# Packed score columns, quarter-wide states and y tiles in a state-space scan with FFN on one core

## The reference

```python
# B=4 sequences, L=512 tokens, D=256; NH=32 heads of HEADDIM=8, D_STATE=64
h = layernorm(x) * (1 + ca) + sa
xBC, z, A_log = split(h @ W_in.T)            # x: 256, B: 32*64, C: 32*64, z: 256, A: 32
xBC = causal depthwise conv of 4 taps (xBC) + conv_b
a = -softplus(A_log)
Lm = exp(segsum(a))                          # lower triangle, per head 512 x 512
M = einsum('blhn,bshn,bhls->bhls', Cm, Bm, Lm)
y = einsum('bhls,bshp->blhp', M, x) + D * x
x = x + ga * ((y * silu(z + z_bias)) @ W_out.T)
h = layernorm(x) * (1 + cb) + sb
x = x + gb * (fwht(silu(h @ W1.T) * (h @ W3.T)) @ W2.T)
```

## Time and profile before

| | us |
|---|---|
| median of 3 runs | 563.15 |
| lowest, highest | 562.98, 563.3 |
| the profiled execution | 562.82 |
| its span, from the first to the last instruction | 561.0 |

### The profile page before, as it was taken

How to read it: one execution, slowest core, us unless ns; L and a number is a source line. 1 busy time by engine, 2 the same in 40 slices (tenths; PEclk the granted TensorE clock), 3 DMA queues, 4 the chain that set the end, 5 groups by cost and what they waited for, 6 DMA issues and landing times.

```text
span 561.0 us, 18569 instructions
## 1 busy us (share of the span) xinstructions
PE 551.6 (98%) x6701; PEld 447.0 (80%) x6702; DVE 471.9 (84%) x746; ACT 392.3 (70%) x988; POOL 256.8 (46%) x523
## 2 busy tenths in 40 slices
PE   7999999999999999999999999999999999999997
PEld 4577787888778878788887888787788988889887
DVE  7899999999999999999999999999948637647343
ACT  2679898898898888988988989988723323333240
POOL 4854387576577577687678364656100000000000
PEclk9899999999999999999999999999999999999999
DMA  8636534433433535533533437456741042100101
GB/s 275 264 140 199 171 120 132 166 117 121 168 117 118 168 112 203 171 113 119 162 127 117 143 142 223 135 163 191 204 136 54 22 129 75 39 2 0 39 1 37
DMA packets 40816, 72.01 MB, mean 128 GB/s; under 512 B 4676, under 2 KB 12100, under 8 KB 40520
## 3 DMA queue, kind: packets, MB, share of 16 engines
q1 hardware_dynamic: 40776, 71.52, 40.0%
HBM read 57.34 MB, written 13.12 MB: 126 GB/s over the span
## 4 chain that ended last, share of the span: by engine, by line
PE 93%; DVE 2%; issue 2%; POOL 1%; DMA 1%; ACT 0%; SPq 0%; POOLq 0%; DVEq 0%; ACTq 0%
PE ps L355 20%; PE ps L357 20%; PE ps L356 20%; PE ps L530 9%; PE ps L512 5%; PE ps L574 5%; PE ps L549 4%; PE ps L565 4%; PE ps L640 2%; PE ps L449 1%; PE ps L377 1%; PE ps L407 1%; PE ps L421 1%; PE ps L650 1%; DMA u_sb<-in_u 1%
## 5 line engine op out<-in xcount | busy, mean ns | idle before, releaser
L1148 DVE SCALAR_TENSOR_TENSOR acc<-ps,cw_dve,acc 128x511 f32<-128x511 f32 (+2 forms) x384 | 257.7, 742 | 2.9 <-ACT acc L807 2.7
L839 ACT ACTIVATE decay<-sums,p_slot 128x128 f32<-128x128 f32 x512 | 161.1, 399 | 4.8 <-POOL sums L1436 2.1
L1432 POOL TENSOR_SCALAR_AFFINE_SELECT sums<-sums 128x512 f32<-128x512 f32 x128 | 82.4, 644 | 93.5 <-DMA sums<-running_sums 88.5
L807 ACT ACTIVATE acc<-ps,cw_act 128x512 f32<-128x512 f32 x128 | 93.1, 776 | 32.2 <-PE ps L574 30.1
L355 PE MATMUL ps<-ht_hi,wg_hi 128*128 128x512 f32 x256 | 107.1, 418 | 0.0
L356 PE MATMUL ps<-ht_lo,wg_hi 128*128 128x512 f32 x256 | 101.2, 395 | 0.0
L357 PE MATMUL ps<-ht_hi,wg_lo 128*128 128x512 f32 x256 | 101.1, 395 | 0.0
L1136 DVE TENSOR_TENSOR mix<-ps,decay 128x1024 f32<-128x1024 f32 x64 | 78.2, 1222 | 11.4 <-PE ps L530 10.2
L974 ACT ACTIVATE silu_sb<-ps 128x512 f32<-128x512 f32 x32 | 19.2, 599 | 77.8 <-PE ps L357 77.8
L1436 POOL TENSOR_SCALAR_AFFINE_SELECT sums<-sums 64x256 f32<-64x256 f32 x128 | 51.9, 405 | 29.7 <-POOL sums L1432 29.2
L1366 POOL TENSOR_TENSOR rstd<-vareps,minus_half 128x4 f32<-128x4 f32 x8 | 8.4, 1047 | 120.4 <-DVE vareps L1030 116.8
(11 more groups left out here) (142 smaller groups left out, 945.2 us busy)
## 6 DMA issues: line engine op xcount, KB each, us to landing
sums<-running_sums SPq DMA_DIRECT2D x128, 256.0 KB, 3.2
y_parts<-yt_sb SPq DMA_DIRECT2D x32, 256.0 KB, 2.0
wg_raw<-in_w_bc SPq DMA_DIRECT2D x8, 512.0 KB, 4.5
stage<-y_parts SPq DMA_DIRECT2D x16, 256.0 KB, 4.5
u_sb<-in_u SPq DMA_DIRECT2D x4, 512.0 KB, 4.3
stage<-in_w SPq DMA_DIRECT2D x1, 2048.0 KB, 13.2
x_channels<-acc SPq DMA_DIRECT2D x8, 256.0 KB, 2.6
ee<-decay_rows SPq DMA_DIRECT2D x8, 256.0 KB, 3.9
```

The costliest lines, as they stand in the source:

```text
L807: af(acc[:, b % 2, t, :], ps[:, PROJ_BANK[t], :], ACT.Identity, bias=cw_act[:, t, 1:2], scale=cw_act[:, t, 0:1]).then_inc(s[f"tap_a{t}"], 1)
L839: i = af(decay[:, j, c * P:(c + 1) * P], sums[:, j, c * P:(c + 1) * P], ACT.Exp, scale=-1.0, bias=p_slot[:, b * CH + c, j:j + 1])
L1148: stt(a[:, d:], ps[:, PROJ_BANK[t], 0:L - d], cw_dve[:, t, TAPS - 1 - d:TAPS - d], a[:, d:], ALU.mult, ALU.add).then_inc(s[f"taps{t}"], 1)
L1432: gp.affine_select(out=v, in_=v, compare_op=ALU.is_ge, fill=FAR, base=0, pattern=[[0, 2], [NS, 2], [1, P]], channel_multiplier=-1).then_in ...
```

## The change

Masks, scores, decays and `mix` take 384 columns a head instead of 512. The first 64 targets of a chunk have only its first 64 sources; the other 64 partitions of their columns were masked. Two chunks, an even and an odd one, now share PW = 192 columns: in partitions 0 to 63 stand first the 64 columns of the odd chunk's second sources, then the 128 of the even chunk's first sources, and in partitions 64 to 127 the same with even and odd exchanged. `sums_d` gets two packed rows of 384 a head, one for each half of the partitions, in four DMAs at the start. What is above the diagonal is always within 64 columns of a half, so a mask is one addition of a constant tile `far_above`, 0 or 3e38, to 256 columns (no select).

y takes 256 columns of bank 7 instead of 512: for a pair of chunks k and a pair of heads p, `intra` writes 32 partitions in quarter 2 k + p, and `inter` 32 in quarter 2 (1 - k) + p, both in columns 128 k to 128 k + 127. So quarters 0 and 1 take two matmuls of `inter`, quarters 2 and 3 one, and each takes four of `intra`. `xs` becomes a row of weight blocks in which a window of 32 columns has the head's x in its place and zeros elsewhere. `inter` takes the states of two heads in one matmul of 32 columns, 6 instead of 12. `intra` has 16 as before, 32 wide, 8 of 128 and 8 of 64 columns. `states` has 24 matmuls on quarters of 32 state rows instead of 12 on halves of 64. `own_x` is four products with a 0/1 column in place of two copies. `store_y` is two DMAs and `load_y` eight, of 128 columns each, instead of two of 512. The matrices `triu`, `strict` and `ones`, which nothing reads, are no longer loaded.

```diff
+PW = P + NS
+PL = CH // 2 * PW
+XW = 4 * QD + HD
+ST0 = [0, 48, 64]
...
+            packed = sums_d.rearrange("(n h) (k m) -> n h k m", h=2, k=2)
+            full = sums_t[:].rearrange("p (k e l) -> p k e l", k=2, e=2)
+            for h in range(2):
+                sp.dma_start(packed[:, h, :, NS:PW], full[:, :, h, :]).then_inc(s["st_sums"], 16)
+                sp.dma_start(packed[:, h, :, 0:NS], full[:, :, 1 - h, NS:P]).then_inc(s["st_sums"], 16)
+            sp.wait_ge(s["st_sums"], 64)
...
-                row = sums_d[bass.ds(b * NH + g * JH + j, 1), :]
-                sp.dma_start(sums[:, j, :], row.to_broadcast([P, L])).then_inc(s[f"ld_sum{j}"], 16)
+                rows = sums_d[bass.ds((b * NH + g * JH + j) * 2, 2), :].unsqueeze(1)
+                sp.dma_start(sums[:, j, 0:PL], rows.to_broadcast([2, NS, PL])).then_inc(s[f"ld_sum{j}"], 16)
 
             def store_y(g, b):
 
                 sp.wait_ge(s["yt_ev"], g * B + b + 1)
-                sp.dma_start(y_d[bass.ds((b * NG + g) * P, P), :], yt_sb[:, b % 2, :]).then_inc(s[f"st_y{b % 2}"], 16)
+                for h in range(2):
+                    rows = y_d[bass.ds(((2 * b + h) * NG + g) * NS, NS), :]
+                    sp.dma_start(rows, yt_sb[NS * h:NS * (h + 1), b % 2, :]).then_inc(s[f"st_y{b % 2}"], 16)
...
             def load_y(b, kt):
 
-                own = y_d[(b * NG + 4 * kt) * P:(b * NG + 4 * kt + 4) * P, :].rearrange("(q r) l -> q r l", r=QD)
-                load(yi[:, kt, :], own[:, 0:HD, :], f"ld_y{kt}")
-                load(yo[:, kt, :], own[:, HD:2 * HD, :], f"ld_y{kt}")
+                for part, dst in enumerate((yi, yo)):
+                    for c in range(CH):
+                        k, r = divmod(c, 2)
+                        first = ((2 * b + (part ^ k)) * NG + 4 * kt) * NS
+                        own = y_d[first:first + 4 * NS, k * P:(k + 1) * P].rearrange("(q r x) l -> r q x l", r=2, x=2 * HD)
+                        load(dst[:, kt, c * P:(c + 1) * P], own[r], f"ld_y{kt}")
...
-                            i = mm(ps[NS * at:NS * (at + 1), 2 + a, c * P + NS * h:(c + 1) * P],
+                            o = c // 2 * PW + NS * (1 - h)
+                            i = mm(ps[NS * at:NS * (at + 1), 2 + a, o:o + P - NS * h],
...
+                        for i4 in range(JH):
+                            j = 2 * p + i4 // 2
+                            own = slice(QD * i4, QD * (i4 + 1))
                             o = ps[own, 6, 3 * P + p * 24 + c * HD:3 * P + (p + 1) * 24]
-                            i = mm(o, b_tok[:, p, c * P + NS * a:c * P + NS * (a + 1)],
+                            i = mm(o, b_tok[:, p, c * P + QD * i4:c * P + QD * (i4 + 1)],
...
-                for c in range(1, CH):
-                    for j in range(JH):
-                        p, a = divmod(j, 2)
-                        mm(ps[QD * j:QD * j + YW, 7, c * P:(c + 1) * P], st_sb[:, p, a, c - 1, :],
-                           acc[:, b % 2, 2 + p, c * P:(c + 1) * P], start=(c == 1), stop=False, skip_group_check=True)
+                for c in (2, 1, 3):
+                    for p in range(2):
+                        k = c // 2
+                        quarter = 2 * (1 - k) + p
+                        mm(ps[QD * quarter:QD * (quarter + 1), 7, k * P:(k + 1) * P], st_sb[:, p, ST0[c - 1]:ST0[c - 1] + QD],
+                           acc[:, b % 2, 2 + p, c * P:(c + 1) * P], start=(c < CH - 1), stop=False, skip_group_check=True)
 
             def intra(q, b):
 
-                pe.wait_ge(s["xs_done"], 2 * q + 2)
+                pe.wait_ge(s["xs_done"], 4 * q + 4)
                 pe.wait_ge(s["mixed"], 2 * q + 2)
-                for c in range(CH):
-                    for j in range(JH):
-                        i = mm(ps[QD * j:QD * j + YW, 7, c * P:(c + 1) * P], xs[:, b % 2, c, j, :],
-                               mix[:, j, c * P:(c + 1) * P], start=False, stop=True, skip_group_check=True)
-                        if c == CH - 1:
-                            i.then_inc(s["intra"], 1)
+                for a in range(2):
+                    for h in range(2):
+                        for k in (1, 0):
+                            for p in range(2):
+                                j = 2 * p + a
+                                quarter = 2 * k + p
+                                w = j * XW - HD * a + (2 * k + h) * QD
+                                i = mm(ps[QD * quarter:QD * (quarter + 1), 7, k * P + NS * h:(k + 1) * P],
+                                       xs[:, b % 2, w:w + QD], mix[:, j, k * PW + NS * (1 - h):k * PW + PW - P * h],
+                                       start=False, stop=True, skip_group_check=True)
+                                if a and h:
+                                    i.then_inc(s["intra"], 1)
...
+                for n in range(CH):
+                    k, h = divmod(n, 2)
+                    own = slice(k * PW + NS * (1 - h), k * PW + PW - P * h)
+                    i = af(decay[:, j, own], sums[:, j, own], ACT.Exp, scale=-1.0, bias=p_slot[:, b * CH + n, j:j + 1])
...
-                nc.scalar.copy(yt_sb[:, half, :], ps[:, 7, :]).then_inc(s["yt_ev"], 1)
+                    act.wait_ge(s[f"st_y{half}"], 32 * before)
+                nc.scalar.copy(yt_sb[:, half, :], ps[:, 7, 0:2 * P]).then_inc(s["yt_ev"], 1)
...
-                tt(mix[:, 2 * p:2 * p + 2, :], ps[:, 2:4, :], decay[:, 2 * p:2 * p + 2, :],
+                tt(mix[:, 2 * p:2 * p + 2, 0:PL], ps[:, 2:4, 0:PL], decay[:, 2 * p:2 * p + 2, 0:PL],
...
+            gp.memset(far_above[:], 0.0).then_inc(s["mask_set"], 1)
+            gp.memset(own_half[:], 0.0).then_inc(s["mask_set"], 1)
+            for h in range(2):
+                rows = slice(NS * h, NS * (h + 1))
+                pool.wait_ge(s["mask_set"], 2 + 2 * h)
+                gp.memset(own_half[rows, h:h + 1], 1.0).then_inc(s["mask_set"], 1)
+                gp.affine_select(out=far_above[rows], in_=far_above[rows], compare_op=ALU.is_ge, fill=FAR, base=0,
+                                 pattern=[[1, NS]], channel_multiplier=-1).then_inc(s["mask_set"], 1)
+            pool.wait_ge(s["mask_set"], 6)
...
-                even = x_tok[:, b * CH:(b + 1) * CH:2, bass.ds(g * GC, GC)]
-                odd = x_swapped[:, b, :, bass.ds(g * GC, GC)]
-                gp.tensor_copy(xs[:, b % 2, 0::2, :, 0:HD], even.rearrange("p c (j e) -> p c j e", j=JH)).then_inc(s["xs_done"], 1)
-                if isinstance(n, int) and n < B:
-                    pool.wait_ge(s[f"ld_xs{b}"], 32)
-                gp.tensor_copy(xs[:, b % 2, 1::2, :, 0:HD], odd.rearrange("p c (j e) -> p c j e", j=JH)).then_inc(s["xs_done"], 1)
+                blocks = xs[:, b % 2, :].rearrange("p (j w) -> p j w", j=JH)[:, :, 0:4 * QD].rearrange("p j (k w) -> p k j w", k=2)
+                for c in range(2):
+                    if c == 0:
+                        x = x_tok[:, b * CH:(b + 1) * CH:2, bass.ds(g * GC, GC)]
+                    else:
+                        x = x_swapped[:, b, :, bass.ds(g * GC, GC)]
+                        if isinstance(n, int) and n < B:
+                            pool.wait_ge(s[f"ld_xs{b}"], 32)
+                    x = x.rearrange("p k (j e) -> p k j e", j=JH)
+                    for h in range(2):
+                        at = QD * h + 2 * HD * c
+                        rows = own_half[:, (h + c) % 2:(h + c) % 2 + 1].unsqueeze(1).unsqueeze(1).to_broadcast([P, 2, JH, HD])
+                        gp.tensor_tensor(blocks[:, :, :, at:at + HD], x, rows, ALU.mult).then_inc(s["xs_done"], 1)
 
             def mask(n, j):
 
                 await_unit(f"ld_sum{j}", 16 * (n + 1))
-                v = sums[:, j, :].rearrange("p (c e l) -> p c e l", c=2, e=2)
-                gp.affine_select(out=v, in_=v, compare_op=ALU.is_ge, fill=FAR, base=0, pattern=[[0, 2], [NS, 2], [1, P]],
-                                 channel_multiplier=-1).then_inc(s["masked"], 1)
-                await_unit("masked", 8 * n + 2 * j + 1)
-                o = v[0:NS, :, 1, :]
-                gp.affine_select(out=o, in_=o, compare_op=ALU.is_ge, fill=FAR, base=-NS, pattern=[[0, 2], [1, P]],
-                                 channel_multiplier=-1).then_inc(s["masked"], 1)
+                v = sums[:, j, 0:PL].rearrange("p (k l) -> p k l", k=2)[:, :, 0:P].rearrange("p k (e l) -> p k e l", e=2)
+                far = far_above[:].unsqueeze(1).unsqueeze(1).to_broadcast([P, 2, 2, NS])
+                gp.tensor_tensor(v, v, far, ALU.add).then_inc(s["masked"], 1)
```

More of the change, by code:

```diff
@@ L61, in adaln_ssm_ffn_kernel @@
         x_tok = sb("x_tok", [P, TT, D], F32)
-        cst = sb("cst", [P, 5, P], F32)
-        ident, triu, strict, ones, hadamard = (cst[:, i, :] for i in range(5))
+        cst = sb("cst", [P, 2, P], F32)
+        ident, hadamard = (cst[:, i, :] for i in range(2))
         wo_sb = sb("wo_sb", [P, KT, D], F32)
@@ L428, in p_transposes @@
                 for c in range(CH):
-                    if c % 2 == 0:
```

(28 more changed lines are left out.)

53 lines of the change are left out of this document (26 added, 27 removed).

## The result

The changed kernel takes **794.35 us** (median of 4 runs, 792.76 to 795.9) against 563.07 us for the kernel before in the same series: a ratio of 1.411 (95% interval 1.4075 to 1.4146). The forecast was 545.7 us, range 539.5 to 554. It is wrong by far, and its sign too. The profiled execution took 792.76 us, its span is 791.0 us.

What follows compares the result with a forecast made beforehand. TensorE was taken as the bound, VectorE and ScalarE close behind. 30 steps x 0.62 = 18.6 us, plus 0.6 in the tail, less 1.8 for loads of y, gave 17.4 us gained: 545.7 us, range 539.5 to 554.

Steps and rivals of the forecast that it cites:

- SP and DMA: SP's queue and transfers: one more y store issue, sums stored in four DMAs, some 2 us later; cost nil.
- rival 3: SP's queue: small y loads take 0.6 us each and land late, costing 8 us instead of 1.8; 552 us, chance 0.08.
- Inter and intra: TensorE's `inter` and `intra` blocks: the busiest quarters go from 1.54 to 1.12 us a step, gain 0.42.
- States: TensorE's `states` block, 24 matmuls for 12: 0.60 us instead of 0.80, gain 0.20 a step; bounds 0.47 and 1.49.
- rival 1: TensorE's `states`: matmul records cost time wherever they go, 29 ns each gives 573 us, 22 ns gives 563; chance 0.09.
- The step: TensorE's step in the loop: from 10.68 to 10.06 us, above VectorE's 9.8 and ScalarE's 8.9.
- VectorE: VectorE's `mix` products, 768 columns for 1024: 0.24 us saved on each, its step falls from 10.3 to 9.8 us.
- rival 2: VectorE or ScalarE bounds the step: if `mix` saves nothing, the step is 10.35 us, the time 554 us; chance 0.13.
- GpSimd: GpSimd's masks and `own_x` products: a mask 0.74 us instead of 1.27, between 2.1 less and 0.9 more together; cost nil.
- Loads of y: More y load issues on SP delay sums and y: 1.3 us at the first place, 0.5 at the third, 1.8 together.
- The start: Before the loop: GpSimd's extra memsets and selects, some 2 us, fit in 3.65 us of idle time; cost nil.
- The sum: Whole kernel: 30 steps give 18.6 us, the tail 0.6, loads of y -1.8; together 17.4 us gained, 545.7 us.

Runs made afterwards that it cites:

- sum_halves: The changed kernel with each load of sums as two DMAs of 64 partitions instead of one with two rows outermost: 551.53 us, ratio 0.981 to the kernel before.
- y_spread: `sum_halves` with the first eight loads of y issued four behind each of two steps, not in a row: 547.37 us, ratio 0.9715 to the kernel before.
- before_two_rows: The kernel before, nothing packed, with each running sum stored twice and loaded with an outermost dimension of 2: 949.14 us in one run, against 562.75.

## Why the prediction was wrong

**The step that failed** is in "SP and DMA" and in the account of the first load of y: the load of the sums was treated as a transfer with 25% fewer bytes, "the transfer 25% smaller". In the sum it is a term of nil: the step of 10.06 us is held against VectorE's 9.8 and ScalarE's 8.9, and against no transfer. The trace of before had 3.2 us for 256 KB from issue to landing, but for a load with 128 entries outermost. The new form, two rows outermost, runs at 48 GB/s: some 4.2 us for 192 KB, four of them 17 us a step where the sum had 10.06. No rival had it either; rival 3 looked at SP's issues, not at how a DMA is spread. The place to stop was in the diff: `[2, NS, PL]` where `[P, L]` had stood. Everything that followed was read from durations of instructions on engines, and the DMA share of 0.44 in the earlier trace rows seemed to say that DMAs had room. It says that of 16 engines together.

The other steps can be judged in `sum_halves` and `y_spread`, where only that cause is gone:
- *Inter and intra* gain 0.42: from 1.65 to 1.22, gain 0.43. Right in size (the working has both sides 0.1 too low, 1.54 and 1.12), and it fits a rate set within a quarter; no run tries that by itself.
- *States*, 0.60, gain 0.20: 0.58, gain 0.22. Right. 48 records in 0.58 us are 12 ns each, so rival 1 and its 22 to 29 ns a record fall. The Trainium skill ("TensorE: Matmul & The Clock Gate", "Wait — 56ns, not 53.3ns?") gives about 25 ns as the least from start to start; taken for each record, as in the prediction, that does not hold across quarters here. Counted by f32 matmuls of two records it is 24 ns, and this trace doesn't contradict it.
- *The step*, 10.06 forecast: 10.04. *VectorE*: `mix` 0.95 us for 0.97, its wait for `scores` is still there, and rival 2 did not come. *GpSimd*: a mask 0.73 to 0.75 for 0.74.
- *Loads of y*, 1.3 us at the first place, bounds 0.5 to 3: 3.9. Mis-sized, and nearer the 3 of rival 3. The issues came 0.65 us apart, not 0.60 or less, and `sum_halves` itself puts one more issue ahead of each sum.
- *The start*: booked at nil. In `sum_halves` two early steps take 12.33 and 10.7 instead of 10.0, as TensorE waits for split weights that stand behind GpSimd's late masks: about 3 us.
- *The sum*: 545.7 with 1.8 for loads of y. `sum_halves` has 551.5: 2.6 more for that load and 2.9 at the early steps are 5.5 of the 5.8. What is left is small only because it cancels. In the profiled executions, apart from these losses, the steps up to the 30th `intra` gain 19.4 us where the sum had 18.6, and the first `intra` starts 0.7 earlier; but from the 30th `intra` to the end it takes 185.1 us instead of 182.8, where the tail and the later loads of y were booked at a gain of 0.1. That `y_spread`, another kernel, comes to 547.4, inside the range given for the change, doesn't make the forecast right.

## What to carry to other kernels

When an edit changes the shape of an access pattern in DRAM or SBUF, price the DMA again, even if its bytes fall: look at the entries of its outermost dimension, not only at the bytes. A low DMA share together with waits for a DMA is no contradiction but the mark of a transfer on few engines, and the fine view (one tenth in every slice, never zero) shows it at a glance. And before giving up the change behind it, split the slow DMA so that each part has many entries outermost: here that turned 41% slower into 1.9% faster.

## What the runs showed of the hardware

- A transfer on few engines delays others that use all of them. From the page of the kernel after, and then of `sum_halves` (KB each, us to landing):

```profile
wg_raw<-in_w_bc SPq DMA_DIRECT2D x8, 512.0 KB, 12.0
y_parts<-yt_sb SPq DMA_DIRECT2D x64, 64.0 KB, 6.8
```
```profile
wg_raw<-in_w_bc SPq DMA_DIRECT2D x8, 512.0 KB, 4.2
y_parts<-yt_sb SPq DMA_DIRECT2D x64, 64.0 KB, 2.0
```

  The same weights and the same stores take three times as long, though the mean DMA share is 0.22. That a part of each queues behind the loads of sums on two busy engines fits the burst of `before_two_rows`, but no run tries it by itself.
- SP's issues also grow: in the kernel after a load of sums occupies its queue for 2.47 us (median), in `sum_halves` for 0.49. Below, their shortest, median and longest duration in ns; in the kernel before the median was 333. Why they grow wasn't tried.

```profile
L233 SPq DMA_DIRECT2D sums<-packed_sums x128: 503/2466/5201, 38.9 to 610.1; - x128
L234 SPq DMA_DIRECT2D sums<-packed_sums x256: 465/488/1962, 39.9 to 376.4; - x128
```

- The granted clock falls with TensorE's waits: mean 0.81 in the loop. After the waits of 6.65 and 4.74 us below it is 0.50 (1.2 GHz) from 313.85 to 317.00 and projections start 0.43 us apart; from 323.00 to 324.50 it is 1.00 (2.4 GHz), and they start 0.23 to 0.24 apart. So work that stands right behind a wait is slower as well.

```profile
308.21 0.90 PE L527 MATMUL ps<-cst,acc 128*128 128x128 f32 x3 [6.65 <-ACT b_tok L854]
313.85 0.80 PE L370 MATMUL ps<-ht_hi,wg_hi 128*128 128x512 f32 x1 [4.74 <-POOL wg_lo L1395]
...
315.30 0.63 PE L370 MATMUL ps<-ht_hi,wg_hi 128*128 128x512 f32 x1
315.73 0.63 PE L371 MATMUL ps<-ht_lo,wg_hi 128*128 128x512 f32 x1
...
323.61 0.40 PE L370 MATMUL ps<-ht_hi,wg_hi 128*128 128x512 f32 x1
323.84 0.39 PE L371 MATMUL ps<-ht_lo,wg_hi 128*128 128x512 f32 x1
```
